# Taking a block's own rows off the neighbour sum: two VectorE subtractions in place of a TensorE matmul

## The reference, cut to what matters

```
h   = max(layernorm(x), 0)
m   = relu(h @ Wm1 + bm1) @ Wm2 + bm2            # a message for every node
agg = segment_sum(m[src], dst)                   # sum of the messages over the listed edges
x   = x + h + relu(concat(h, agg) @ Wn1 + bn1) @ Wn2 + bn2
```

## Time and profile before

| | |
|---|---|
| median of 3 runs | 4332.27 us (4330.55 to 4336.07) |
| profiled execution | 4333.03 us, of which the span 4331.3 us |
| TensorE matmul, busy in the span | 3169.1 us (73%) |
| TensorE weight load | 2934.3 us (68%) |
| VectorE | 2500.2 us (58%) |
| ScalarE | 2150.0 us (50%) |
| GpSimd | 2354.1 us (54%) |

### The profile page before, as it was taken

How to read it: one execution, slowest core, us unless ns; L and a number is a source line. 1 busy time by engine, 2 the same in 40 slices (tenths; PEclk the granted TensorE clock), 3 DMA queues, 4 the chain that set the end, 5 groups by cost and what they waited for, 6 DMA issues and landing times.

```text
span 4331.3 us, 88730 instructions
## 1 busy us (share of the span) xinstructions
PE 3169.1 (73%) x27093; PEld 2934.3 (68%) x27093; DVE 2500.2 (58%) x11435; ACT 2150.0 (50%) x3978; POOL 2354.1 (54%) x2044
## 2 busy tenths in 40 slices
PE   3555555333333466676997649999999999999999
PEld 2344333222222365565997639999999999999999
DVE  7766666444444799997223123477666555555444
ACT  1222222111111355555997639866555666666665
POOL 3677777777777888888888888532111000000111
PEclk8555555555555699998999779999999999999999
DMA  4999997555555699995997749835666777777886
GB/s 133 357 375 360 371 362 213 142 136 136 136 140 137 172 235 232 234 233 103 235 252 176 164 92 241 232 111 158 228 227 229 237 255 255 242 257 251 264 276 229
DMA packets 628728, 954.72 MB, mean 220 GB/s; under 512 B 192650, under 2 KB 451057, under 8 KB 623152
## 3 DMA queue, kind: packets, MB, share of 16 engines
q1 hardware_dynamic: 451824, 840.25, 59.5%
q0 software_dynamic: 171904, 107.02, 14.6%
q10 hardware_dynamic: 4544, 1.77, 0.2%
HBM read 754.44 MB, written 194.32 MB: 219 GB/s over the span
## 4 chain that ended last, share of the span: by engine, by line
PE 39%; POOL 38%; issue 12%; DMA 8%; DVE 2%; SPq 1%; ACT 0%; POOLq 0%; DVEq 0%; ACTq 0%
PE ps L1097 31%; POOL adj L723 23%; POOL rows L715 15%; DMA adj<-count,place 3%; PE ps L1143 2%; DMA h_rows<-rows 2%; PE ps L1094 2%; DMA rows<-table,src_of 2%; PE ps L1152 1%; DMA spare_sum<-key_list 1%; PE ps L1155 1%; PE ps L1116 1%; DMA pieces<-adj 0%; PE ps L1129 0%; DMA x<-in_x 0%
## 5 line engine op out<-in xcount | busy, mean ns | idle before, releaser
L1097 PE MATMUL ps<-tab,wide 128*128 128x256 f32 x14616 | 1883.9, 287 | 149.7 <-DVE summed_f L1535 128.0
L1097 PEld LDWEIGHTS ps<-tab,wide 128*128 128x128 f32 x14616 | 1796.4, 192 | 156.0 <-DVE summed_f L1535 132.3
L901 ACT CAST wide<-pieces 128x896 fp32r<-128x896 f16 x1497 | 1344.5, 939 | 544.8 <-PE ps L1097 378.8
L723 POOL DMA_INDIRECT adj<-count,place x832 | 1316.2, 1582 | 258.1 <-issue 244.8
L715 POOL DMA_INDIRECT rows<-table,src_of x880 | 846.1, 961 | 314.1 <-issue 258.7
L1675 DVE CAST wide<-pieces 128x896 fp32r<-128x896 f16 x603 | 368.7, 624 | 251.0 <-PE ps L1097 244.3
L757 POOL DMA_DIRECT2D out<-x_rows x49 | 26.7, 545 | 889.6 <-DVE x_rows L1640 881.7
L1347 DVE SCALAR_TENSOR_TENSOR same<-spare_sum,key,ps 128x128 bf16<-128x128 f32 x832 | 283.5, 342 | 359.7 <-DMA spare_sum<-key_list 359.7
L1011 PE MATMUL ps<-dst_mlp,onehot_t 128*128 x2640 | 367.5, 232 | 148.3 <-DVE pre L1383 84.8
L1025 PE MATMUL ps<-weight_parts,onehot_b 128*128 128x4 bf16 x880 | 131.1, 184 | 424.0 <-DVE weight_parts L1410 407.5
L1025 PEld LDWEIGHTS ps<-weight_parts,onehot_b 128*128 128x128 bf16 x880 | 91.5, 104 | 501.6 <-issue 480.1
(11 more groups left out here) (261 smaller groups left out, 4057.8 us busy)
## 6 DMA issues: line engine op xcount, KB each, us to landing
pieces<-adj SPq DMA_DIRECT2D x527, 448.0 KB, 4.3
pieces<-adj SPq DMA_DIRECT2D x297, 672.0 KB, 5.5
h_rows<-rows SPq DMA_DIRECT2D x220, 256.0 KB
rows<-h_rows SPq DMA_DIRECT2D x220, 256.0 KB
spare_sum<-key_list SPq DMA_DIRECT2D x104, 512.0 KB
pieces<-adj SPq DMA_DIRECT2D x155, 224.0 KB, 2.8
onehot_list<-onehot_b SPq DMA_DIRECT2D x220, 128.0 KB
low_row<-low_list SPq DMA_DIRECT2D x220, 128.0 KB
```

Of the source, the lines that this page charges most:

```text
L723: nc.gpsimd.indirect_dma_start(out=adj[:, :], out_offset=bass.IndirectOffsetOnAxis(ap=place[:, k:k + 1], axis=0), in_=count16[:, k:k + 1], ...
L901: nc.scalar.copy(to, of).then_inc(cast_act, 1)
L1097: last = nc.tensor.matmul(ps_sum[u % 3], of, tab[q % 2][:, c, :, :].rearrange("p t d -> p (t d)"), start=(c == u0), stop=(kind in ("spare" ...
```

## The change

In the third dense pass the matmul with `neg_ident` goes, and with it the tile, its semaphore and the instruction that made it. VectorE reduces the sum into `summed_f`, subtracts from it the high part of the unit's own rows (waiting for that result), then the low part, and writes `source`. TensorE's transposes wait for the second subtraction (`sourced`) where they waited for the reduction.

```diff
@@ -304,7 +304,6 @@
         tab = [tab_0, tab_1]
         pieces = sb("pieces", [P, AR, PIECE_C, P], f16)
         wide = sb("wide", [P, SUB_RING, SUB, P], f32r)
-        neg_ident = sb("neg_ident", [P, P], f32r)
         x_rows = sb("x_rows", [P, XR, D])
         spare_parts = sb("spare_parts", [P, HALVES, D], f32r)
         summed_f = sb("summed_f", [P, D])
@@ -471,7 +470,6 @@
         x_new = sem("x_new")
         merged = sem("merged")
         reduced = sem("reduced")
-        neg_set = sem("neg_set")
         spare_set = sem("spare_set")
         sourced = sem("sourced")
         d_turned = sem("d_turned")
@@ -1100,10 +1098,6 @@
 
             def add_spare(u):
                 q, w = UNITS[u][:2]
-                if LAYER[q]["kind"] == "update":
-                    pe.wait_ge(neg_set, 1)
-                    nc.tensor.matmul(ps_sum[u % 3], neg_ident[:, :], tab[q % 2][:, w, :, :].rearrange("p t d -> p (t d)"),
-                                     start=False, stop=False)
                 pe.wait_ge(spare_set, spares(u))
                 if UNITS[u][4] == "late":
                     nc.tensor.matmul(ps_sum[u % 3][:, 0:D], ident[:, :], acc[:, w, :], start=False, stop=False)
@@ -1120,7 +1114,7 @@
                 n = q * DB + w
                 after(pe, d_turned_sb, n)
                 if LAYER[q]["kind"] == "update":
-                    pe.wait_ge(reduced, UNIT_OF[q, w] + 1)
+                    pe.wait_ge(sourced, n + 1)
                     pe.wait_ge(acc_set, w + 1)
                     nc.tensor.transpose(ps_turn[:, 0, :], acc[:, w, :], ident[:, :])
                     nc.tensor.transpose(ps_turn[:, 1, :], source[:, 1, :], ident[:, :]).then_inc(d_turned, 1)
@@ -1513,7 +1507,6 @@
             roots = [0]
 
             link(nc.vector.memset(slots[:, :, :].bitcast(f32), 0.0))
-            nc.vector.tensor_scalar(neg_ident[:, :], ident[:, :], -1.0, None, ALU.mult).then_inc(neg_set, 1)
 
             def measure_block(at):
                 link(nc.vector.bn_stats(stats_d[:, :], at))
@@ -1573,7 +1566,9 @@
                 after(dve, d_turned, q * DB + w)
                 inv = dinv[:, 1, w:w + 1]
                 if kind == "update":
-                    reduce_sum(u, source[:, 1, :])
+                    reduce_sum(u, summed_f[:, :])
+                    link(nc.vector.tensor_tensor(summed_f[:, :], summed_f[:, :], tab[q % 2][:, w, 0, :], ALU.subtract))
+                    nc.vector.tensor_tensor(source[:, 1, :], summed_f[:, :], tab[q % 2][:, w, 1, :], ALU.subtract).then_inc(sourced, 1)
                 elif kind == "gcn1":
                     reduce_sum(u, summed_f[:, :])
                     nc.vector.tensor_scalar(source[:, 0, :], summed_f[:, :], inv, None, ALU.mult).then_inc(sourced, 1)
```

## The result

The changed kernel is slower, by 0.5%. Its median is 4356.61 us beside 4333.12 for the kernel before, ratio 1.0050, 95% interval [1.0038, 1.0062]. A second series gave 4353.29 beside 4334.11, ratio 1.0045 [1.0031, 1.0059]. The forecast was 4352, slower.

What follows compares the result with a forecast made beforehand. The bound was a loop through TensorE, VectorE's chain and ScalarE's copy. 47 x 0.535 = 25.1, plus 0.3, less 5.9, gave +19.5 us on 4333.03 or 4332.27, said as 4352 us; range 4344 to 4360.

Steps and rivals of the forecast that it cites:

- Neither path has slack, delay passes one to one: Third pass: TensorE's own work and ScalarE's copy reach the up-projection within 0.01 us; VectorE 0.22 late made TensorE 0.24 late.
- The matmul is worth 0.12 us per block on the other leg: Between up-projection and closing on TensorE: removing 49 matmuls shortens the 2.68 us leg, 5.9 us gained.
- The pair costs 0.535, the second one with an unlinked step: VectorE's two subtractions after the reduce: between 0.52 and 0.65 us; the second isn't followed by a wait for its result.
- Rival B: VectorE's pair: both subtractions take full steps, 0.65 us together, +25.1 us, 4357.4 us; chance 17%.
- Period 8.085, +19.5 us: Third-pass block: legs of 5.525 and 2.56 us, period 8.085 where it was 7.67; +19.5 us in total.
- Moved wait and casts hidden: TensorE's transposes wait for the second subtraction with 1.4 us to spare; VectorE's first cast, half a microsecond later, stays hidden.
- The up-projection waits in 47 blocks, 24 us in total: TensorE's up-projection load waits for ScalarE's copy, about 0.5 us in each block, where the total was 0.5 us.
- VectorE's wait shrinks to 1.9, ScalarE's grows to 2.9: Per block, VectorE's wait for the closing matmul goes from 2.00 us, ScalarE's for the variance from 2.50 us.
- The last block pays about 0.3: Last third-pass block: ScalarE's cast is shorter, so 0.24 us of the pair's 0.535 is covered.
- Rival A: TensorE's saving alone: the pair vanishes in VectorE's waiting, the matmuls' 5.9 us remain, 4326.4 us; chance 7%.
- Rival C: TensorE's clock falls to 0.52 for a tenth of the pass because of gaps: 18 us more, 4370 us; chance 4%.
- the copy can't pass the two casts ahead of it: ScalarE works its list in order, so its copy's end is tied to VectorE's chain, with no time between.

Runs made afterwards that it cites:

- add_only: Kernel before, matmul kept, VectorE's two subtractions added and the transposes waiting for the second: 4362.38 us beside 4334.19, ratio 1.0066.
- before_copy_early: Kernel before, with ScalarE's copy of the turned source issued ahead of its second cast in the third pass: 4334.60 us beside 4334.19, ratio 1.0003.
- remove_only: Kernel before, with the negative-identity matmul left out and nothing put in its place: 4327.35 us beside 4334.19, ratio 0.9983.
- second_held: Changed kernel, with VectorE also waiting for the second subtraction's result before going on: 4359.87 us beside 4334.11, ratio 1.0066.
- changed_copy_early: Changed kernel, with ScalarE's copy of the turned source issued ahead of its second cast in the third pass: 4326.22 us beside 4334.19, ratio 0.9986.

## Why the prediction was right

- *Neither path has slack, delay passes one to one.* Right. add_only paid 0.52 per block of a pair of 0.53; the closing-to-projection leg grew from 4.99 to 5.52, forecast 5.525. The prediction had this from one late block and one pair of times; add_only and before_copy_early show it for the whole pass.
- *The matmul is worth 0.12 us per block on the other leg.* Right: 2.55 measured, 2.56 forecast, and 5.8 us in remove_only for 5.9.
- *The pair costs 0.535, the second one with an unlinked step.* Right: 0.53, L1621 0.21 us after L1571. Rival B is refuted as a description of this kernel, though its 4357.4 lay nearer to the first median than the forecast: B's own kernel, second_held, has a pass 6.3 us or more longer.
- *Period 8.085, +19.5 us.* Slightly high: 8.07, and +18.45 in the pass. About half of the 1 us between is that four blocks before, but one after, ran late (0.76 us together against 0.25); the other half is 0.01 us per block. The first median, 4356.61, is 4.6 us above the forecast and 5 us above what the pass gives, for no reason that the prediction or a profile shows.
- *Moved wait and casts hidden.* Right: TensorE comes to L1119 at 3149.94, 1.4 us after the second subtraction's end at 3148.55, and no wait for it or for one of VectorE's casts is listed in the pass.
- *The up-projection waits in 47 blocks, 24 us in total.* Right: 48 blocks, 22.9 us.
- *VectorE's wait shrinks to 1.9, ScalarE's grows to 2.9.* Right: 91.0 / 49 = 1.86 and 140.6 / 49 = 2.87.
- *The last block pays about 0.3.* Right: its leg is 5.22 us (3394.14 - 3388.92) where it was 4.97 (3376.54 - 3371.57), so 0.25.
- *Rival A* needed 0.415 us of cover, and the kernel before had none. It came true as soon as the copy was moved: 4326.22 us in changed_copy_early, 4326.4 in the prediction. *Rival C* did not come: clock 1.00 in the pass with TensorE's loads idle 6% of it.

What the prediction left unused is its own remark that the copy can't pass the two casts ahead of it. The cost lies as much in that order as in VectorE's chain: moving the copy ahead of one cast turns the change from a loss into a small gain.

## What to carry to other kernels

An engine's idle time says that work can be given to it, not where. Before moving work from a full engine to an idle one, follow the loop that passes through both: an instruction put ahead of a result that the full engine needs costs its whole step in each turn if that path has no slack (0.52 us here), one put behind that result may cost almost nothing (0.08). Where a wait is absent, look how near it is: compare the time at which the operand is ready with the time at which its user would have come by its own work.

## What was not expected

Some blocks, counted by the closing that they begin with, run late by 0.1 to 0.4 us. The 18th is late in all ten profiles: between the 18th and the 19th closing ScalarE's first cast starts 0.34 to 0.35 us after the root, where 0.11 is the rule. The distance between these closings was 7.91 us before, 8.32 in both profiles of the changed kernel, 7.79 in remove_only and 8.44 in add_only, against 7.67, 8.07 or 8.08, 7.55 and 8.19 as a rule. The other late blocks lie elsewhere from kernel to kernel (the 20th, 31st and 42nd before and in remove_only, the 3rd, 19th and 35th in add_only), and in these VectorE's variance is late, by 0.1 to 0.3 us; the block of the earlier trace rows is the 20th. In changed_copy_early and before_copy_early the same cast of the 18th block is late too, but its distance is as long as the others (7.54 and 7.66): the cover swallows the delay. What makes these instructions late was not tried.
